# Mamba scan in a four-layer kernel: six of 32 units multiply with B on ScalarE, transposed, and TensorE turns the product into PSUM

## The reference

```python
rn = resid * rsqrt(mean(resid * resid, -1) + EPS) * norm_w
x = silu(conv(rn @ in_w.T))                    # 512 channels e, 4 taps
delta = softplus(x @ wd1.T @ wd2.T + wd2_b)
A = -exp(A_log); Bm = x @ wB.T; Cm = x @ wC.T  # 16 states n
def step(h, inp):
    d_l, b_l, c_l, x_l = inp
    h = exp(d_l[:, :, None] * A) * h + (d_l * x_l)[:, :, None] * b_l[:, None, :]
    return h, einsum('ben,bn->be', h, c_l)
y = (scan(step) + x * W_D) * silu(rn @ skip_w.T)
resid + y @ out_w.T
```

## Time and profile before

| | before |
|---|---|
| median of 3 runs | 1888.03 us (1887.62 to 1890.15) |
| profiled execution | 1887.28 us |
| its span | 1885.6 us |
| TensorE busy, weight loads busy | 1742.8 us (92%), 1381.1 us (73%) |
| VectorE busy | 1432.4 us (76%) |
| ScalarE busy | 1079.3 us (57%) |
| GpSimd busy | 1060.5 us (56%) |

### The profile page before, as it was taken

How to read it: one execution, slowest core, us unless ns; L and a number is a source line. 1 busy time by engine, 2 the same in 40 slices (tenths; PEclk the granted TensorE clock), 3 DMA queues, 4 the chain that set the end, 5 groups by cost and what they waited for, 6 DMA issues and landing times. The chain is left out here.

```text
span 1885.6 us, 26501 instructions
## 1 busy us (share of the span) xinstructions
PE 1742.8 (92%) x9613; PEld 1381.1 (73%) x9613; DVE 1432.4 (76%) x2198; ACT 1079.3 (57%) x1866; POOL 1060.5 (56%) x633
## 2 busy tenths in 40 slices
PE   6888989899898989877899999999999899999999
PEld 2456666666556566655788888888888688888888
DVE  4899999999999999999777566666355755655665
ACT  6777787877777786787433433334444443334433
POOL 3889999999999999999722101112445411110111
PEclk9898999999999999988999999999999999999999
DMA  6223233233333233253000000000000000000000
GB/s 197 84 80 107 95 105 97 87 111 96 97 97 105 95 104 101 91 170 98 1 1 1 1 1 1 1 23 6 1 0 0 1 12 12 12 12 12 12 11 12
DMA packets 59109, 101.40 MB, mean 54 GB/s; under 512 B 11120, under 2 KB 11248, under 8 KB 58864
## 3 DMA queue, kind: packets, MB, share of 16 engines
q1 hardware_dynamic: 58992, 99.88, 16.6%
HBM read 95.14 MB, written 4.72 MB: 53 GB/s over the span
## 5 line engine op out<-in xcount | busy, mean ns | idle before, releaser
L383 POOL TENSOR_TENSOR m_U<-m_U,m_C 128x1024 f32<-128x1024 f32 x255 | 600.8, 2369 | 25.7 <-DVE m_U L890 15.5
L525 PEld LDWEIGHTS m_y<-ident,m_U 128*128 128x128 f32 x2048 | 252.6, 148 | 118.0 <-issue 70.9
L890 DVE TENSOR_TENSOR_SCAN m_U<-m_dA,m_carry,m_U 128x512 f32<-128x512 f32 x256 | 310.6, 1263 | 5.1 <-ACT m_dA L758 4.8
L525 PE MATMUL m_y<-ident,m_U 128*128 128x128 f32 x2048 | 284.8, 285 | 30.3 <-POOL m_U L383 30.2
L890 DVE TENSOR_TENSOR_SCAN m_U<-m_dA,m_U 128x512 f32<-128x512 f32 x256 | 295.9, 1203 | 11.5 <-ACT m_dA L758 8.2
L758 ACT ACTIVATE m_dA<-high,m_negA 128x512 f32<-128x512 f32 x256 | 172.3, 685 | 71.5 <-DVE m_U L890 71.1
L758 ACT ACTIVATE m_dA<-even,m_negA 128x512 f32<-128x512 f32 x256 | 170.7, 684 | 54.0 <-DVE m_U L890 53.0
L1123 POOL TENSOR_TENSOR SW<-g_Rt 128x1024 f32<-128x1024 f32 x16 | 31.6, 1996 | 252.6 <-ACT g_Rt L1308 252.6
L1123 POOL TENSOR_TENSOR SW<-f_Rt 128x1024 f32<-128x1024 f32 x16 | 31.6, 1995 | 205.2 <-ACT f_Rt L1308 205.2
L1303 ACT ACTIVATE g_sil<-g_psG 128x512 f32<-128x512 f32 x96 | 57.4, 598 | 140.2 <-PE g_psG L1181 139.6
L1303 ACT ACTIVATE f_sil<-f_psG 128x512 f32<-128x512 f32 x96 | 57.4, 598 | 134.9 <-PE f_psG L1181 134.2
(11 more groups left out here) (375 smaller groups left out, 4316.0 us busy)
## 6 DMA issues: line engine op xcount, KB each, us to landing
m_C<-bc_rows SPq DMA_DIRECT2D x256, 256.0 KB, 3.2
m_B<-bc_rows SPq DMA_DIRECT2D x60, 256.0 KB, 3.5
even<-in_ffn_w SPq DMA_DIRECT2D x16, 256.0 KB, 5.0
out<-res SPq DMA_DIRECT2D x8, 512.0 KB, 2.8
res<-in_x SPq DMA_DIRECT2D x1, 3072.0 KB, 13.0
res<-in_x SPq DMA_DIRECT2D x2, 512.0 KB, 4.3
turned<-in_Wkvqu SPq DMA_DIRECT2D x1, 1024.0 KB, 4.7
high<-in_in_w SPq DMA_DIRECT2D x1, 512.0 KB, 4.3
```

The source lines that it names most:

```text
L383: pool.tensor_tensor(u, u, C[:, M % C_RING, :].unsqueeze(1).to_broadcast([P, PE_E, CHUNK]), ALU.mult).then_inc(hc_ready, 1)
L525: last = nc.tensor.matmul(y[:, t, j * P:(j + 1) * P], U[:, M % U_RING, j, t * P:(t + 1) * P], ident[:, :], start=False, stop=n == N - 1, i ...
L890: nc.vector.tensor_tensor_scan(u, dA[:, s % A_RING, :], u, carry[:, e, n:n + 1] if q else 0.0, ALU.mult, ALU.add).then_inc(scan_done, 1)
```

## The change

In chunks 1 to 7, six units a chunk are **turned**: 5, 9, 12 of the first pass and 1, 3, 15 of the second (units 17, 19, 31). For these the product with B is made with time on the partitions. Jobs "tr0" to "tr3" transpose dx of a chunk into `dxT`, "bt" the rows of B into `BT`, both through the `job` banks and a copy by ScalarE. `product(M)` on ScalarE is then four activations (one per 128 tokens) of 128x256 with a scale per partition, two iterations ahead of the unit, behind that iteration's decays; `turn_product` on TensorE transposes it, four tiles per block, into the `dA` buffer of the unit's decay, and the decay itself goes to `dAT` in SBUF. The first block's turn stands at the head of TensorE's iteration, ahead of the row of B, the second behind the parts. The scan reads both and writes `U`.

GpSimd's units become (3, 7, 14) and (6, 9, 12) in odd chunks, (3, 7, 14) and (6, 11) in even chunks from 2; chunk 0 keeps its own. The ring of C has three rows, that of B one, asked for two units ahead. The DMAs of the feed-forward weights begin one unit later in the last chunk, and two conversions of them on ScalarE move from iterations 21 and 26 to 26 and 28.

```diff
-    U_RING, C_RING, A_RING, B_RING = 6, 8, 3, 2
-    ON_POOL, AHEAD = ((3, 7, 10, 14), (4, 9, 14), (3, 7, 11, 14), (3, 6, 10, 14)), 3
+    U_RING, C_RING, A_RING = 6, 3, 3
+    ON_POOL, AHEAD, B_AHEAD = [((3, 7, 10, 14), (4, 9, 14))] + [((3, 7, 14), (6, 9, 12)), ((3, 7, 14), (6, 11))] * 4, 3, 2
+    TURNED, TURN_AHEAD = [((), ())] + [((5, 9, 12), (1, 3, 15))] * (CHUNKS - 1), 2
...
+        dxT = sb("dxT", [P, KE, TILES, P])
+        BT = sb("BT", [P, TILES, N])
+        dAT = sb("dAT", [P, PE_E, CHUNK])
...
-                 5: ("cv1", "back3"), 6: ("cv1+",), 7: ("in2",), 8: ("cv2",), 9: ("cv2+",), 10: ("in3",),
+                 5: ("cv1", "back3"), 6: ("cv1+", "tr2"), 7: ("in2",), 8: ("cv2",), 9: ("cv2+", "tr3"), 10: ("in3",),
...
-                 27: ("out1",), 28: ("out1+",), 29: ("back0",), 30: ("back1",),
+                 27: ("out1",), 28: ("out1+", "tr0"), 29: ("back0",), 30: ("back1",), 31: ("tr1", "bt"),
...
+                if M + B_AHEAD in pool_units:
+                    n_b = place(M + B_AHEAD)[3]
+                    assert n_b >= B_AHEAD
+                    need(sp, pool_mult, POOL_BEFORE[M + B_AHEAD])
+                    sp.dma_start(B[:, :], bc_rows[q, n_b:n_b + 1, :].to_broadcast([P, CHUNK])).then_inc(B_ready, 16)
...
+            def turn_product(M, j):
+
+                s = PE_E * M + j
+                pe.wait_ge(UT_ready, TURNED_BEFORE[M] + 1)
+                pe.wait_ge(scan_done, s - A_RING + 1)
+                for t in range(TILES):
+                    last = nc.tensor.transpose(dA[:, s % A_RING, t * P:(t + 1) * P],
+                                               U[:, M % U_RING, j, t * P:(t + 1) * P], ident[:, :])
+                last.then_inc(UT_turned, 1)
...
             for M in range(ALL_UNITS):
-                if M + 2 < ALL_UNITS and M + 2 not in pool_units:
+                if M + 1 in turned_units:
+                    turn_product(M + 1, 0)
+                if M + 2 in dve_units:
                     spread_B(M + 2)
                 for name, k in parts_of(PE_AT, M):
                     part(name, k)
+                if M + 1 in turned_units:
+                    turn_product(M + 1, 1)
...
+            def product(M):
+
+                c, q, p, n = place(M)
+                for e in range(PE_E * p, PE_E * (p + 1)):
+                    wait_freed(act, f"tr{e}", c)
+                wait_freed(act, "bt", c)
+                act.wait_ge(nsum_done, M - U_RING + 1)
+                for t in range(TILES):
+                    last = nc.scalar.activation(U[:, M % U_RING, :, t * P:(t + 1) * P], dxT[:, pair(p), t, :], ACT.Copy,
+                                                scale=BT[:, t, n:n + 1])
+                last.then_inc(UT_ready, 1)
...
                     decay(PE_E * (M + 1) + 1)
+                if M + TURN_AHEAD in turned_units:
+                    product(M + TURN_AHEAD)
...
+                decay, product = dA[:, s % A_RING, :], u
+                if M in turned_units:
+                    dve.wait_ge(UT_turned, PE_E * TURNED_BEFORE[M] + j + 1)
+                    decay, product = dAT[:, j, :], dA[:, s % A_RING, :]
...
-                nc.vector.tensor_tensor_scan(u, dA[:, s % A_RING, :], u, carry[:, e, n:n + 1] if q else 0.0,
+                nc.vector.tensor_tensor_scan(u, decay, product, carry[:, e, n:n + 1] if q else 0.0,
```

More of the change, by code:

```diff
@@ L151, in mamba @@
         B_full, rows_ready, rows_out = sem("B_full"), sem("rows_ready"), sem("rows_out")
-        B_ready, pool_mult = [sem(f"B_ready{i}") for i in range(B_RING)], sem("pool_mult")
+        B_ready, pool_mult = sem("B_ready"), sem("pool_mult")
+        UT_ready, UT_turned = sem("UT_ready"), sem("UT_turned")
         C_ready = [sem(f"C_ready{i}") for i in range(C_RING)]
@@ L191, in mamba @@
         BEHIND = {"out0": -1, "out0+": -1, "out1": -1, "out1+": -1, "gate1": -1, "back2": -1, "back3": -1,
-                  "gate0": 0, "back0": 0, "back1": 0, "silu_g": 0, "sum": 2, "square": 2, "factors": 2, "norm": 2, "double": 2}
+                  "gate0": 0, "tr2": 0, "tr3": 0, "back0": 0, "back1": 0, "silu_g": 0, "sum": 2, "square": 2, "factors": 2, "norm": 2, "double": 2}
         ASKED = dict(enumerate((4, 1, 5, 0), CHUNKS))
@@ L199, in parts_of @@
             late = [(name, k) for slot, name, k in at["late"] if c == CHUNKS - 1 and slot == i]
-            chunks = [(name, k) for name, k in chunks if 0 <= k < CHUNKS and (name, k) != ("back1", CHUNKS - 1)]
+            chunks = [(name, k) for name, k in chunks if 0 <= k < CHUNKS and (name, k) != ("back1", CHUNKS - 1)
+                      and (k > 0 or name[:2] != "tr")]
             return chunks + late
@@ L239, in place, with before @@
             return c, c % 2, i // N, i % N
-        pool_units = [M for M in range(ALL_UNITS) if M % N in ON_POOL[M // N % (2 * PASSES)]]
-        BEFORE = [len([m for m in pool_units if m < M]) for M in range(ALL_UNITS)]
+        pool_units = [M for M in range(ALL_UNITS) if M % N in ON_POOL[M // UNITS][M // N % PASSES]]
+        turned_units = [M for M in range(ALL_UNITS) if M % N in TURNED[M // UNITS][M // N % PASSES]]
+        dve_units = [M for M in range(ALL_UNITS) if M not in pool_units and M not in turned_units]
+        def before(units):
+            return [len([m for m in units if m < M]) for M in range(ALL_UNITS + 1)]
+        POOL_BEFORE, TURNED_BEFORE, DVE_BEFORE = before(pool_units), before(turned_units), before(dve_units)
         def pair(p):
@@ L443, in part @@
                     last = mm(take(name, k), [(rnT[:, d, t:t + P], skw[:, d, :]) for d in range(KD)])
+                elif name[:2] == "tr":
+                    e = int(name[2])
+                    pe.wait_ge(dx_ready, KE * k + e + 1)
+                    out = take(name, k)
+                    for t in range(TILES):
+                        last = nc.tensor.transpose(out[:, t * P:(t + 1) * P], dx[q][:, e, t * P:(t + 1) * P],
+                                                   ident[:, :])
+                elif name == "bt":
+                    pe.wait_ge(rows_ready, k + 1)
+                    out = take(name, k)
+                    for t in range(TILES):
+                        last = nc.tensor.transpose(out[:, t * 2 * N:(t + 1) * 2 * N], rows[:, t * P:(t + 1) * P],
+                                                   ident[0:2 * N, 0:2 * N])
                 elif name[:2] == "cv":
@@ L504, in spread_B @@
                     wait_freed(pe, "bc", c)
-                need(pe, mult_done, M - BEFORE[M])
+                need(pe, mult_done, DVE_BEFORE[M])
                 nc.tensor.matmul(psB[:, :], pick[:, n:n + 1].to_broadcast([P, P]), stack[:, q, :], start=True,
                                  stop=True).then_inc(B_full, 1)
+            def turn_product(M, j):
+                s = PE_E * M + j
+                pe.wait_ge(UT_ready, TURNED_BEFORE[M] + 1)
+                pe.wait_ge(scan_done, s - A_RING + 1)
+                for t in range(TILES):
+                    last = nc.tensor.transpose(dA[:, s % A_RING, t * P:(t + 1) * P],
+                                               U[:, M % U_RING, j, t * P:(t + 1) * P], ident[:, :])
+                last.then_inc(UT_turned, 1)
             def nsum(M):
@@ L908, in _ @@
             for M in range(ALL_UNITS):
-                if M + 1 < ALL_UNITS and M + 1 not in pool_units:
+                if M + 1 in dve_units:
                     mult(M + 1)
```

48 lines of the change are left out of this document (26 added, 22 removed), and 4 rows, old and new, of the table ACT_AT.

## The result

| | before | changed |
|---|---|---|
| median | 1888.42 us (4 runs) | 1906.03 us (1905.46 to 1909.92, 4 runs) |
| ratio | | 1.0096, 95% interval 1.0081 to 1.0111 |
| profiled span | 1885.6 us | 1903.7 us |
| TensorE, weight loads busy | 1742.8, 1381.1 us | 1771.9, 1412.5 us |
| VectorE, ScalarE, GpSimd busy | 1432.4, 1079.3, 1060.5 us | 1406.9, 1152.7, 1031.0 us |

The change made the kernel 18 us (0.96%) slower, where 7 us less were forecast and the range ended at 1900. The answer to the earlier trace rows is the busy time by windows of the changed kernel: chunks 2, 3 and 7, then the first half of chunk 3 and the second half before it (columns as in the earlier trace rows).

What follows compares the result with a forecast made beforehand. VectorE, GpSimd and TensorE were taken as nearly full, TensorE's order using up the first half's gain. Chunks 1 to 6 -4.2 us, chunk 7 -4.4 and +1.5: together -7, so 1881 us; range 1858 to 1900.

Steps and rivals of the forecast that it cites:

- VectorE and GpSimd, 31 us if all of it counts.: Chunks 1 to 7: VectorE loses 28 products, 31 us, GpSimd 14, 33 us; the kernel 31 us faster if all counted.
- TensorE's first half, 52.5 us without a wait.: From pass 0's skip products to pass 1's, TensorE's work in order sums to 52.5 us, against 52.2 and 52.7 before.
- First half: +0.7 us: Each first half of chunks 1 to 6: only unit 5's late product holds TensorE up, 0.7 us; the other four cost nothing.
- Second half: -1.4 us.: Pass 1's skip products to the next chunk's: VectorE -1.1, faster start -0.9 on average, unit 31's product 0.6 late.
- The gain of 1.7 "in even chunks": Second half's start: the product after the skip products comes 1.7 us sooner in even chunks, 0.2 in odd ones.
- Chunk 7: -3 us.: Last chunk: four VectorE products less, -4.4 us, and 1.5 back for waits between ScalarE and TensorE; about 3 us shorter.
- Rings cost nothing.: Shorter rings of C and B rows cost nothing; in the last chunk a late C row at most 1 us each.
- Product 1.8 us.: ScalarE's four activations of 128x256 per turned unit were taken as 1.8 us.
- TensorE has room: Rival: TensorE's iterations overlap more closely, VectorE stays the bound and 31 us come out whole, 1857 us; chance 22%.
- The clock: Rival: added transposes keep TensorE's lower clock two units longer, VectorE waits 2 us a chunk, 1893 us; chance 13%.
- The product comes late: Rival: TensorE, then VectorE, stall for ScalarE's turned product, 0.5 us for each of 42 units, 1902 us; chance 15%.
- 16 us spare a chunk: ScalarE's waits for VectorE, about 16 us a chunk, were taken as its real spare time against 13 us added work.

Runs made afterwards that it cites:

- e13: Changed kernel without the turned units' products with B, turns, tr0 to tr3 and bt, so only VectorE's and GpSimd's relief: 1857.80 us, ratio 0.9843 to the kernel before.
- e16: e13 plus TensorE's load (eight transposes per turned unit) and ScalarE's (four activations each), nobody waiting for either: 1875.13 us, ratio 0.9932.
- e18: e16 with tr0 to tr3, bt and their copies by ScalarE kept, nobody waiting for a product or turn: 1888.96 us, ratio 1.0003.
- e4: Changed kernel with two of the four taps of the convolution left out: 1884.15 us, ratio 0.9977 to the kernel before.
- e5: Kernel before the change with the same two of four convolution taps left out: 1885.78 us, ratio 0.9985.
- e14: e13 plus only TensorE's load, eight 128x128 transposes per turned unit that nobody waits for: 1869.27 us, ratio 0.9910.
- e15: e13 plus only ScalarE's load, four activations of 128x256 where each product stands, nobody waiting: 1868.80 us, ratio 0.9897.
- e1: Changed kernel with job tr2 and its copy one iteration later, on the other bank: 1902.09 us, ratio 1.0062 to the kernel before.
- e10: e3 plus only ScalarE's load, four activations of 128x256 where the six products stand, nobody waiting: 1894.80 us, ratio 1.0034.
- e3: Changed kernel with no turned units, transposes of dx and B left out, old GpSimd units; short rings and later weight DMAs stay: 1888.04 us, ratio 0.9997.

## Why the prediction was wrong

The account from 1888 to 1906 by these runs: the relief -30.3 (e13), the loads of TensorE and ScalarE +17.3 (e16), the transposes and copies of dx and B with tr2's wait +13.8 (e18), waiting for products and turns +17.1 (by subtraction). The terms are medians; by the traces the third is 10.9.

The forecast was 25 us off between the two traces (-7 against +18). Of these, 6 x 2.7 = 16 lie in the first halves, 6 x 0.4 = 2 in the second ones and 7 in chunk 7; chunk 0 and what follows chunk 7 make up -1.

- *VectorE and GpSimd, 31 us if all of it counts.* Right: 30.3. Both the count of products and their price held.
- *TensorE's first half, 52.5 us without a wait.* Right. In chunk 3 the half is 55.9 us; the rows and the distances around them show 0.55 at unit 5, 1.0 at tr2, 1.2 at unit 17, and two of 0.2: the turn of unit 9 starts at 406.56, when its product ends (406.51), and "cv3" at 417.02, when ScalarE's copy of "in3" ends (416.93). All 3.15 us are waits for ScalarE, and leave 52.7. The Trainium skill (Perfetto Trace Analysis, Identifying the Most-Contended Engine) would take the busy share of weight loads, 69.9 of 108.5 us here, for a TensorE with room. e4 against e5 speaks against that rule in this stage: the same 6.9 us a chunk were worth 22 us in one kernel and 2 in the other.
- ***First half: +0.7 us* is the step that failed.** It measured +3.4 in each of six chunks. I counted only unit 5's wait (0.7; 0.55 measured). I called the other four "asked for late enough, because TensorE is the last". That was argued with ScalarE on time. But TensorE, being late, delays "cv3" on ScalarE (0.97 us in e14, 0.74 here), this the SiLU of x, this both the decays and the product of unit 17; e14 against e13 shows it up to the decays, and ScalarE's own load does as much to them (e15). And I did not follow the banks: with tr2 put between "back3" and "in2" it takes the bank of "cv1" of its own iteration, so that TensorE and ScalarE wait for each other in turn; e1 shows what this cost, 6.2 us in the six chunks.
- *Second half: -1.4 us.* Measured -1.0. The gain of 1.7 "in even chunks" was read from the one second half of 55.4 us behind chunk 2's first; those of chunks 4 and 6 took 53.8 before.
- *Chunk 7: -3 us.* Measured +4.4, of which up to 3 can be scatter. The relief is worth 2.7 us there and not 4.4 (e13), and with it ScalarE's load alone costs 6.7 (e15), 7.8 without (e10), so I had 1.5 where it took 7. TensorE waits 14.6 us for products, in six places. The longest, unit 9:

```profile
838.82 0.69 ACT L808 ACTIVATE m_dA<-high,m_negA 128x512 f32<-128x512 f32 x1 [1.61 <-DVE m_U L958]
839.45 1.69 ACT L819 ACTIVATE m_U<-m_dxT,m_BT 128x256 f32<-128x256 f32 x4
```

```profile
841.19 1.11 PE L542 MATMUL m_dA<-ident,m_U 128*128 128x128 f32 x4 [3.46 <-ACT m_U L819]
```

ScalarE itself had been idle for 1.61 us: the product stands behind a decay that waits for a scan. The product ahead of that iteration's decays was not tried.
- *Rings cost nothing.* Right (e3). One wait of 1.1 us for a row of C appears in the last chunk.
- *Product 1.8 us.* 1.69.
- *The rivals.* "TensorE has room" is out (e4, and e14, where TensorE's load alone costs 11.5 us); its 1857 is what the relief gives without any load (e13). "The clock" is out: the clock was 1.00 where it had been 0.95 and 0.96. The rule of the Trainium skill (TensorE: Matmul & The Clock Gate, Part 4: PE-mode transpose) that transposes don't count as work for the clock did not show here: with 67 and 61 more records, nearly all transposes, no window of chunks 2 and 3 is at the lower level. "The product comes late" was the nearest, with 1902 us: up to 17 us of waits against its 21. It added them to the forecast, though, and had nothing for tr2 and the copies (e18). I gave it 15% for the "16 us spare a chunk", and a mean of spare time says nothing on a product that stands behind 4.5 us of SiLU and table loads.

## What to carry to other kernels

When an engine's own order is nearly full, count for each added job which buffer it takes and whose copy frees that buffer, and walk the chain of both engines once around; a share of idle time does not show whether work in a fixed order comes in time. Measure a shift of work in three parts: the relief alone, the loads with nobody waiting, then the waits; here they are -30, +31 and +17 us. A small dose in the places where the helper is free (two units in chunks 1 to 6, tr2 on the other bank and the urgent instruction first) kept 8 us where six units lost 18.

## What the runs showed of the hardware

Four activations of 128x256 from SBUF to SBUF with a scale pointer take 1.69 us, 0.40 us from start to start, against 2.06 with scale and bias pointers. A scan with the decay in SBUF and the product in PSUM takes 1.208 us (1.268 with the carry), the usual one 1.203 (1.263): exchanging the two sources costs 5 ns.
